# Value weights centred behind the first mix, one semaphore per swap of the low rank, new order lists

## The reference

```python
xa = _ln(x, ln1_w, ln1_b)
sx = concatenate([state[:, 1:2] - xa[:, :1], xa[:, :-1] - xa[:, 1:]], axis=1)      # the shift
xxx = tanh((xa + sx * maa_x) @ maa_w1).reshape(b, l, 5, DM)                         # first mix, low rank
xxx = einsum('blfd,fde->blfe', xxx, maa_w2)
xm = xa[:, :, None] + sx[:, :, None] * (maa_stack + xxx)                            # five mixes
w = exp(-exp(time_decay + tanh(xw @ td_w1) @ td_w2))
r, k, v = xr @ Wr.T, xk @ Wk.T, xv @ Wv.T
g = silu(xg @ Wg.T)
# over the 128 tokens, for each of 32 heads of 16: a = k v^T; out = r (u a + s); s = a + w s
og = group_norm(out) * gn_w + gn_b
x1 = x + og * g @ Wo.T
xc = _ln(x1, ln2_w, ln2_b); sx2 = shift of xc
rr = sigmoid((xc + sx2 * ffn_maa_r) @ Wfr.T); kk = square(relu((xc + sx2 * ffn_maa_k) @ Wfk.T))
x = x1 + rr * (kk @ Wfv.T)
```

## Time and profile before

| | |
|---|---|
| median of three runs | 931.6 us (928.16 to 932.55) |
| the profiled execution | span 929.8 us, from the first to the last instruction |
| PE busy | 861.4 us, 93% |
| DVE busy | 681.4 us, 73% |
| POOL busy | 537.9 us, 58% |
| ACT busy | 397.8 us, 43% |
| mean granted clock of PE | 0.976 of full |

### The profile page before, as it was taken

How to read it: one execution, slowest core, us unless ns; L and a number is a source line. 1 busy time by engine, 2 the same in 40 slices (tenths; PEclk the granted TensorE clock), 3 DMA queues, 4 the chain that set the end, 5 groups by cost and what they waited for, 6 DMA issues and landing times.

```text
span 929.8 us, 12242 instructions
## 1 busy us (share of the span) xinstructions
PE 861.4 (93%) x4388; PEld 377.5 (41%) x4388; DVE 681.4 (73%) x875; ACT 397.8 (43%) x819; POOL 537.9 (58%) x571
## 2 busy tenths in 40 slices
PE   2799998999989998999899989999979999899998
PEld 1233433343334433334343434444334444445454
DVE  5435599799998999899879999899995434523441
ACT  3022422343245223323245453753456353846495
POOL 1001577778878699799699998888983201010100
PEclk9799999899989999999899999999999999999999
DMA  8082479552766729364655135436020312010102
GB/s 295 11 140 100 135 192 163 166 148 69 156 150 152 222 81 199 107 188 107 170 170 125 45 93 114 139 78 168 19 75 12 91 34 69 1 45 1 45 1 46
DMA packets 93951, 100.46 MB, mean 108 GB/s; under 512 B 22850, under 2 KB 64066, under 8 KB 91842
## 3 DMA queue, kind: packets, MB, share of 16 engines
q1 hardware_dynamic: 86978, 87.09, 37.8%
q10 hardware_dynamic: 6912, 12.59, 3.9%
HBM read 65.05 MB, written 33.55 MB: 106 GB/s over the span
## 4 chain that ended last, share of the span: by engine, by line
PE 62%; POOL 14%; DVE 10%; issue 4%; DMA 4%; ACT 4%; SPq 2%; ACTq 0%; POOLq 0%; DVEq 0%
PE PS L1369 44%; PE PS L1609 4%; POOL VB L756 4%; PE PS L1498 4%; POOL VB L748 3%; POOL VB L752 3%; DMA scr_v<-STG 3%; PE PS L1436 2%; PE PS L1586 2%; PE PS L1378 2%; DVE M L1079 2%; DVE VB L1195 2%; DVE VB L1076 1%; SPq L500 1%; DVE SX L1076 1%
## 5 line engine op out<-in xcount | busy, mean ns | idle before, releaser
L1369 PE MATMUL PS<-M,W 128*128 128x512 f32 x544 | 270.0, 636 | 19.8 <-DVE M L1079 11.7
L1369 PEld LDWEIGHTS PS<-M,W 128*128 128x128 f32 x544 | 102.6, 200 | 158.0 <-issue 136.5
L1195 DVE TENSOR_TENSOR_SCAN VB<-PS,VB 128x512 f32<-128x512 f32 x128 | 149.1, 1206 | 17.7 <-POOL VB L756 14.2
L748 POOL TENSOR_TENSOR VB<-KR,VB 128x1008 f32<-128x1008 f32 x64 | 129.4, 2022 | 55.3 <-PE PS L1498 51.2
L756 POOL TENSOR_TENSOR VB<-VB 128x1008 f32<-128x1008 f32 x64 | 149.8, 2341 | 3.4
L1076 DVE TENSOR_TENSOR VB<-VB,PS 128x2048 f32<-128x2048 f32 x64 | 145.9, 2279 | 1.1
L638 POOL TENSOR_SCALAR NM<-MV 128x2 f32<-128x2 f32 (+1 forms) x24 | 5.8, 243 | 230.0 <-DVE MV L1326 140.8
L752 POOL TENSOR_TENSOR VB<-WG,VB 128x1008 f32<-128x1008 f32 x64 | 128.6, 2010 | 0.0
L1369 PE MATMUL PS<-W,M 128*128 128x512 f32 x224 | 103.9, 596 | 0.0
L1344 DVE TENSOR_REDUCE SM<-PS 128x1 f32<-128x512 f32 x64 | 43.1, 686 | 53.1 <-PE PS L1609 52.4
L1498 PE MATMUL PS<-VB,HEAD 128*32 128x512 f32 x512 | 68.8, 610 | 4.0 <-DVE VB L1076 4.0
(11 more groups left out here) (179 smaller groups left out, 1296.9 us busy)
## 6 DMA issues: line engine op xcount, KB each, us to landing
VB<-scr_vs SPq DMA_DIRECT2D x64, 256.0 KB, 7.3
W<-in_w SPq DMA_DIRECT2D x8, 1024.0 KB, 10.0
scr_vs<-STG SPq DMA_DIRECT2D x64, 64.0 KB, 5.6
scr_v<-STG SPq DMA_DIRECT2D x16, 256.0 KB, 6.4
scr_w<-STG ACTq DMA_DIRECT2D x16, 256.0 KB, 4.8
scr_k<-STG ACTq DMA_DIRECT2D x16, 256.0 KB, 2.0
KR<-scr_k SPq DMA_DIRECT2D x16, 256.0 KB, 3.5
WG<-scr_w SPq DMA_DIRECT2D x16, 256.0 KB, 5.7
```

Of the source, the lines that this page charges most:

```text
L748: po.tensor_tensor(vo, KO[:, 0:N2 - 1].unsqueeze(1).to_broadcast([P, S, N2 - 1]), VB[:, 2 + s, 0, :, 1:N2], ALU.mult).then_inc(g_kv, 1)
L1195: sc = dv.tensor_tensor_scan(s_, PS[:, 5, :], b_, 0.0, ALU.mult, ALU.add)
L1369: mm = pe.matmul(o, l, r, start=i == 0, stop=i == 3)
```

## The change

Four things, in the code below:

- `centre_wv` comes behind the first quarter's `first_mix`, no longer between `sums_a` and `shift_a`.
- Each of the four copies of a swap has a semaphore of its own, `d_xr[f]`, which gains 16 in each quarter; the product of mix f waits for its own copy.
- The five order lists are new from the first steps on. The number of steps of each stream is the same as before on every engine. Their heads are shown, and the one other line of `ORDER_PE` that matters below.
- In the new SP list the head reads, written out: the first loads, copies 1 and 2, the load of the states, copy 3, the 20 stores of v, copy 4, the second quarter's x, the one element, the first batch's loads.

```diff
 ORDER_PE = (
-    "a:16 l:2 a:4 m:3 p:7 a:1 p:2 a:1 p:1 m:1 p:1 a:1 p:5 m:4 a:1 p:1 m:2 p:1 m:1 p:3 m:1 p:6 m:1 p:6 m:1 "
...
-    "c:3 l:1 c:5 l:1 c:1 l:3 end:1 l:1 c:2 l:3 c:2 l:1 c:2 l:9 scan:1 l:6 c:12 scan:1 c:1 l:1 end:1 l:1 "
...
+    "a:16 l:2 a:4 m:3 p:4 m:1 p:4 a:1 p:7 m:3 p:1 m:1 p:1 a:3 m:2 p:1 m:1 p:6 m:1 p:6 m:1 p:4 m:1 p:4 a:1 "
...
+    "c:2 l:3 c:1 l:1 c:1 l:1 c:4 end:1 c:5 l:4 c:1 l:1 scan:1 l:14 c:5 end:1 scan:1 c:7 l:2 c:1 scan:1 "
...
 ORDER_ACT = (
-    "a:9 l:2 p:5 a:1 p:15 a:2 p:5 a:5 p:1 end:1 a:1 p:4 scan:2 p:4 a:1 scan:4 p:1 scan:1 a:1 end:1 p:2 "
...
+    "a:8 l:2 a:1 p:7 a:1 p:13 a:1 p:3 a:2 end:1 p:2 a:1 p:1 a:1 p:1 a:1 p:1 scan:1 a:1 p:1 a:1 p:1 scan:1 "
...
 ORDER_DVE = (
-    "a:7 end:2 a:12 m:7 end:1 m:15 a:3 m:1 a:1 m:1 a:2 m:1 end:1 m:1 a:2 m:4 end:1 m:2 end:1 a:6 scan:1 "
...
+    "a:1 end:1 a:4 end:2 a:3 end:1 a:11 m:19 a:3 m:3 a:1 m:1 a:4 m:1 end:2 m:8 a:6 scan:1 p:1 scan:5 p:1 "
...
 ORDER_POOL = (
-    "k:2 a:1 k:1 a:4 k:1 a:2 k:1 a:1 k:2 a:6 k:2 a:1 scan:5 k:1 scan:20 end:3 scan:2 end:4 scan:1 end:6 "
...
+    "a:1 k:1 a:3 k:3 a:2 k:1 a:8 k:1 scan:1 k:2 a:1 k:1 scan:3 k:1 scan:18 end:5 scan:2 end:4 scan:1 end:3 "
...
 ORDER_SP = (
-    "a:20 p:1 load:1 p:7 load:1 p:12 a:1 load:5 a:1 p:1 a:3 load:2 x:1 p:1 load:1 p:2 load:1 p:2 l:1 p:2 "
...
+    "a:18 load:1 a:1 p:20 a:2 load:5 a:1 p:1 a:1 load:2 p:1 a:2 load:3 p:22 load:1 a:1 load:4 end:1 load:3 "
...
@@ -340,7 +337,7 @@
-        d_xr = sem("d_xr")
+        d_xr = [sem(f"d_xr{f}") for f in range(4)]
@@ -486,7 +483,7 @@
                     for f in range(4):
-                        sp.dma_start(low_rank(f, 1), low_rank(f, 0)).then_inc(d_xr, 16)
+                        sp.dma_start(low_rank(f, 1), low_rank(f, 0)).then_inc(d_xr[f], 16)
                         yield
@@ -1167,10 +1164,10 @@
                     yield from sums_a(q)
+                    yield from shift_a(q)
+                    yield from first_mix(q)
                     if q == 0:
                         yield from centre_wv()
-                    yield from shift_a(q)
-                    yield from first_mix(q)
@@ -1428,7 +1425,7 @@
                     else:
-                        w.wait_ge(d_xr, 64 * (q + 1))
+                        w.wait_ge(d_xr[f], 16 * (q + 1))
```

## The result

| | before | after |
|---|---|---|
| median | 932.08 us (4 runs, 928.16 to 933.14) | 957.58 us (4 runs, 957.18 to 960.6) |
| ratio | 1 | 1.0289 [1.0264, 1.0315] |
| span of the profiled execution | 929.8 us | 955.5 us |

What follows compares the result with a forecast made beforehand. PE, busy 93% of the span and close to full after the start, was taken as the bound. Terms -2.2 - 1.9 - 0.2 - 0.3 - 0.3 = -4.9 us, from 931.6 to 926.7 us; range 919.5 to 935.

Steps and rivals of the forecast that it cites:

- Bounds of the kernel: Whole kernel: PE close to full after the start; in the middle, order counts on PE, DVE and POOL.
- Step 1: Start: centring moved behind the first mix lets DVE's shift and PE's low rank begin earlier, -2.2 us.
- Step 2: First swap: the first product waits only for its own copy instead of all four, -1.9 us.
- Copy 4: First swap: last copy, queued behind the v stores, lands near 69.5; price taken 0, upper bound 1.5 us.
- Step 3 and 4: Start: small moves of POOL and DVE steps, -0.2 us; PE's granted clock around the swap, -0.3 us.
- rival B: More gain: clock stays up or returns earlier, or lane steps fill middle idle; about 921.5 us; chance 0.22.
- Step 5: New order lists: fewer PE steps ahead of the last scan's read-out; -0.3 us, bounds -5 and +9.
- D: Slower: POOL waits longer for PE's scan read-outs before filling value buffers, 12.5 us; about 939 us; chance 0.14.
- three signs named as fatal: First value store not some 4 us earlier; lead gone at POOL's first L748; POOL's read-out wait up over 5 us.
- PE idle from 177 to 700: Middle stretch, where the scans run: PE's idle time was to stay near 27 us.

Runs made afterwards that it cites:

- e3: The kernel before with only the centring moved behind the first mix; 924.32 us, 0.9986 of the kernel before.
- e2: The kernel before with only one semaphore per copy of the swap; 922.0 us, 0.9953 of the kernel before.
- e1: The changed code with the five old order lists; 920.99 us, 0.9961 of the kernel before.
- p2: Changed code, new lists, DVE's large steps of two SBUF tensors replaced by steps reading one, so not computing the reference; 900.92 us, 0.9735 of before.
- p1: Changed code, old lists, DVE's large steps of two SBUF tensors replaced by steps reading one, so not computing the reference; 923.81 us, 0.9986 of before.
- e5: Separate kernel running DVE and POOL steps alone and side by side; with two SBUF inputs DVE's takes 1777 ns instead of 744, POOL's 2638 instead of 2304.
- e4: The changed kernel with eight added POOL waits for DVE's mixes or shifts; 945.35 us, 1.0208 of the kernel before.
- s1: The changed kernel with every large POOL step of the scans cut in two; 938.31 us, 1.0152 of the kernel before.
- s3: The changed code with old lists and every large POOL step of the scans cut in two; 933.72 us, 1.0093 of the kernel before.

## Why the prediction was wrong

- **Bounds of the kernel.** Right where it says that behind the start the order on three engines counts and that an order can lose there what the start gains. It left out that two of the three slow each other down. The sentence ahead of it that the engines meet only through semaphores is wrong by the same rows: DVE and POOL meet without one.
- **Step 1, centring.** Right: 2.2 us at the start in e3. Its worth in the whole kernel, 1.3 us, is not told apart from 0 or from 2.2 (interval -2.7 to +0.1 us).
- **Step 2, semaphores.** Right: 1.9 us at the first product in e2; e2 as a whole came out at -4.3 us (interval -5.8 to -2.9), more than the term. I did not follow the rest. Copy 4, behind the stores on its queue, was issued at 59.97, landed 4.9 us later, and its reader waited 1.45 us for it, to 64.89; the first two copies of that swap took 2.0 each, and the forecast had 5.3 from issue to landing. The ring order of the Trainium skill ("DMA: Bandwidth & Descriptors", section "Queues, rings and completion order"), which the prediction drew on, fits this. PE then still waited 0.66 us for ACT's decay, so the copy cost nothing, as taken.
- **Step 3 and 4.** Terms of 0.2 and 0.3 us, below what the runs resolve. The clock did come back earlier, as rival B had it: the granted clock reads 0.60 from 36 to 41 us and 1.00 from 41 to 46, where it came back at 45.0. No run shows what that was worth. The first eight low-rank records took 5.5 to 6.7 us in the different kernels, in line with the scatter that the prediction allowed for; no kernel was traced twice. Steps 1 and 2 were to give 4.1 us and gave 3.6 (e1).
- **Step 5, the new lists: the step that failed.** Forecast -0.3 us with bounds -5 and +9. Measured about +30. I counted steps ahead of steps and gave each the same duration in any order; the collision of DVE with POOL stood in the sum at nothing, without a reason. Without the collisions the order is worth -22.9 us (p2 against p1), so even the favourable bound was too small; the meetings turn that into +30, a swing of some 53 us (50 by the profiled stretch of the scans). That is a difference between two pairs of kernels and not one reading.
- **The rivals.** D said "slower" and had the wrong mechanism: POOL's wait grew 12.4 us, its price was 12.5, and the loss was more than twice that. The direction held a chance of 0.14. Of the three signs named as fatal, POOL's wait did grow by more than 5 us, though p1 shows that it can without a loss. The other two didn't appear as written: the first value store is 4.4 us earlier, and at POOL's first L748 the lead is 6.75 us. It is gone at DVE's first scan, 2.4 us later than before. PE idle from 177 to 700 (48.4 us for 27) was the sign that told.
- **What I should have read.** The four mixes of the old trace at 102.18, 4.48 us for what takes 2.7 alone, and the group M<-SX,VEC,EXT at a mean of 820 ns where its median is 746, beside PS<-PS,VEC,SX at 749. A mean above the median in the one group, and none in its neighbour with a PSUM operand, points at the resource before any run. What it costs it doesn't say: in the old lists it was nothing (p1).

One case shows the whole chain of effects. At the first c stage PE's idle before the mixes' readers was 4.61 us. DVE before, then DVE, POOL and PE in the changed kernel, in order of time:

```profile
451.29 4.72 DVE L1079 SCALAR_TENSOR_TENSOR M<-SX,VEC,EXT 128x512 f32<-128x512 f32 x7
```

```profile
456.99 12.90 DVE L1076 SCALAR_TENSOR_TENSOR M<-SX,VEC,EXT 128x512 f32<-128x512 f32 x7
...
466.04 2.65 POOL L753 TENSOR_TENSOR VB<-VB 128x1008 f32<-128x1008 f32 x1
...
469.95 1.22 PE L1366 MATMUL PS<-M,W 128*128 128x512 f32 x1 [8.82 <-DVE M L1076]
```

The same run of seven mixes took 4.72 us before, when POOL did only steps of 32 columns beside it. Now four of POOL's large steps lie beside it, it takes 12.9, and PE idles 8.82 us.

No complete version here beats e1 and e2 (0.4 and 0.5% under the kernel before). What stays open is a complete kernel that gets near the 900.9 us of p2. Two ways to try are the mixes' second operand out of the SBUF, and a planner that knows the price of a meeting; neither was tried.

## What to carry over

Before you change which steps of two engines run side by side, compare each group's mean with its time alone; a group that is longer only beside one other engine has a price that belongs to the pair, and a list that ignores it can lose more than it gains. Steps with two SBUF inputs on VectorE are better put into the gaps of GpSimd's large steps (e4 gained 0.8% so) or given one operand from PSUM (shown in e5 alone). Test an order and its collisions apart: here the new order was good, and the meetings hid it.

## What the hardware showed that I had not expected

- VectorE's steps with two SBUF inputs and GpSimd's tensor_tensor take turns. A VectorE step of 128x512, 0.69 to 0.75 us alone, takes up to 2.82 us beside a 128x1008 one and ends about 0.55 us after it (after, e5); a GpSimd step that starts inside a VectorE step takes 0.45 us more than alone (2.75 for 2.30 in e5). In the changed kernel, where several can fall on one step, the products went from 2.00 to at most 2.98 us and the sum from 2.33 to at most 3.18.
- Beside a GpSimd tensor_scalar of 128x1008 the VectorE step took 1.51 us and didn't wait for the end (e5).
- GpSimd instructions of 128x32 cost VectorE next to nothing (752 ns against 744), but themselves take 0.70 us beside such steps and 0.25 behind them (e5).
- One operand in PSUM frees both engines: 744 and 2311 ns side by side, 744 and 2304 alone (e5).
- A GpSimd tensor_tensor cut in two takes 0.18 us more in all: 2 x 1089 ns for 1997 (s1, s3, p2).
- The same meetings cost nothing in one order of the steps and some 50 us in another (e1 and p1, after and p2).
